# Attention scores of one block as two products of 64 rows and 256 columns, in halves of two PSUM banks

## What is computed

```
D      = exp(log_D - max_log_D)          # log_D from cumulated gates, lower triangle only
qk     = einsum('bhsd,bhtd->bhst', q, k / sqrt(32))
C      = qk * D
h      = (C / (max(|sum C|, exp(-max_log_D)) + 1e-6)) @ v
x      = x + head_layernorm(h) * weight
```

## Time and profile before

| | |
|---|---|
| median of 3 runs | 730.92 us |
| profiled execution | 726.55 us, span 724.8 us |
| TensorE matmul busy | 624.0 us, 86% |
| VectorE busy | 475.6 us, 66% |
| ScalarE busy | 316.1 us, 44% |
| GpSimd busy | 328.0 us, 45% |
| first and last score product (L1180) start | 79.8 us, 289.6 us |

### The profile page before, as it was taken

One profiled execution on the slowest core, in us unless ns is written; L12 is line 12 of the kernel. 1 busy time (PEld: TensorE's weight loads), 2 busy tenths in 40 slices (PEclk: granted clock), 3 DMA queues, 4 the chain that ended last, 5 costly groups with the idle time before them and its releaser, 6 DMA issues.

```text
span 724.8 us, 14827 instructions
## 1 busy us (share of the span) xinstructions
PE 624.0 (86%) x3464; PEld 484.7 (67%) x3481; DVE 475.6 (66%) x943; ACT 316.1 (44%) x704; POOL 328.0 (45%) x328
## 2 busy tenths in 40 slices
PE   3873699999999999613299999999999999999993
PEld 1331366677677666511178888888888888888883
DVE  3664367677656636889657676776777676676673
ACT  3453445355344324300045555545555555555551
POOL 2223534536336433217535555555555455455542
PEclk9997699799689658655599999999999999999998
DMA  9995554555645632260113333333333333333332
GB/s 272 294 297 173 158 159 152 177 158 164 183 124 160 182 99 87 79 259 0 30 32 60 59 47 57 59 47 56 59 50 53 59 51 52 59 51 52 59 45 23
DMA packets 71530, 76.70 MB, mean 106 GB/s; under 512 B 12686, under 2 KB 63636, under 8 KB 71508
## 3 DMA queue, kind: packets, MB, share of 16 engines
q1 hardware_dynamic: 55508, 50.20, 22.3%
q0 software_dynamic: 15712, 25.73, 19.6%
q10 hardware_dynamic: 288, 0.52, 0.2%
HBM read 53.21 MB, written 23.21 MB: 105 GB/s over the span
## 4 chain that ended last, share of the span: by engine, by line
PE 76%; DVE 8%; issue 5%; DMA 5%; POOL 2%; ACT 2%; SPq 1%; DVEq 0%; ACTq 0%; POOLq 0%
PE bank L1282 10%; PE bank L1284 9%; PE bank L1283 9%; PE bank L1180 9%; PE bank L1194 7%; PE bank L1314 5%; PE bank L1310 5%; PE bank L1311 5%; PE bank L1297 4%; PE bank L1175 3%; DMA qT_scratch<-qt 3%; PE bank L1177 2%; PE bank L1269 2%; PE bank L1243 2%; PE bank L1211 1%
## 5 line engine op out<-in xcount | busy, mean ns | idle before, releaser
L1102 POOL DMA_INDIRECT out_rows<-ys,index x71 | 112.9, 1590 | 155.7 <-DVE ys L987 151.9
L1282 PE MATMUL bank<-w12l,xh 128*128 x284 | 120.8, 425 | 2.2 <-DVE xl L959 2.2
L1284 PE MATMUL bank<-w12h,xh 128*128 x284 | 112.5, 396 | 0.0
L1283 PE MATMUL bank<-w12h,xl 128*128 x284 | 112.5, 396 | 0.0
L993 DVE TENSOR_TENSOR w3l<-w,w3h 128x1024 fp32r<-128x1024 f32 x71 | 87.2, 1228 | 30.8 <-issue 29.9
L1194 PEld LDWEIGHTS bank<-aug,c 128*128 128x128 f32 x512 | 77.1, 216 | 36.5 <-issue 31.4
L788 DVE SCALAR_TENSOR_TENSOR c<-bank,d 128x512 f32<-128x512 f32 x64 | 44.2, 690 | 75.1 <-PE bank L1194 66.8
L662 ACT CAST w3h<-w 128x1024 fp32r x71 | 74.4, 1048 | 20.0 <-issue 20.0
L1093 POOL DMA_INDIRECT xg<-token_table,index x71 | 70.4, 991 | 23.8 <-issue 21.0
L1180 PE MATMUL bank<-qbd,kt 128*128 128x512 f32 x128 | 78.2, 697 | 3.4 <-issue 3.4
L1310 PE MATMUL bank<-w3l,hth 128*128 128x256 f32 x284 | 76.4, 302 | 1.8 <-DVE w3l L993 1.8
(11 more groups left out here) (165 smaller groups left out, 1128.2 us busy)
## 6 DMA issues: line engine op xcount, KB each, us to landing
x<-in_x SPq DMA_DIRECT2D x32, 256.0 KB, 3.0
wst<-in_w12T POOLq DMA_DIRECT2D x26, 256.0 KB, 3.5
aug<-in_ctxv SPq DMA_DIRECT2D x16, 264.0 KB, 3.0
ct<-in_ctxT SPq DMA_DIRECT2D x16, 256.0 KB, 4.6
qT_scratch<-qt SPq DMA_DIRECT2D x16, 256.0 KB, 3.7
kt<-in_ctxT SPq DMA_DIRECT2D x16, 256.0 KB
qbd<-qT_scratch SPq DMA_DIRECT2D x64, 64.0 KB
out_rows<-x SPq DMA_DIRECT2D x16, 256.0 KB, 2.2
```

Of the source, the lines that this page charges most:

```text
L1102: q.indirect_dma_start(out=out, out_offset=bass.IndirectOffsetOnAxis(ap=index[:, j:j + 1], axis=0), in_=YS[o][:], in_offset=None, compute_ ...
L1282: mm(acc, XH[i][:, k, :], wl, start=(k == 0), stop=False)
L1283: mm(acc, XL[i][:, k, :], wh, start=False, stop=False)
L1284: ins = mm(acc, XH[i][:, k, :], wh, start=False, stop=(k == NK - 1))
```

## The change

Banks 2 and 3 become one tensor `bank23` of two banks. The scores of a block are two fp32 products: rows 0 to 63 (heads 0 and 1 of the group) with the 256 columns of these heads, into the first half of bank 2, and rows 64 to 127 with the other 256 columns into the first half of bank 3. What is left out of the old product was zero by the block diagonal. Every block uses the same two halves, so the scores of block k now wait for the combine of block k-1. The combine reads both halves in one instruction.

```diff
-        bank = [stack.enter_context(nc.psum_tensor(f"bank{i}", [P, 512], F32)) for i in range(8)]
+        bank = [stack.enter_context(nc.psum_tensor(f"bank{i}", [P, 512], F32)) for i in range(2)]
+        bank23 = stack.enter_context(nc.psum_tensor("bank23", [P, 2, 512], F32))
+        bank += [bank23[:, 0, :], bank23[:, 1, :]]
+        bank += [stack.enter_context(nc.psum_tensor(f"bank{i}", [P, 512], F32)) for i in range(4, 8)]
...
-                        v.scalar_tensor_tensor(C[n % 2][:], bank[2 + n % 2][:], KS, D[n % 2][:],
+                        v.scalar_tensor_tensor(C[n % 2][:].rearrange("p (r q) -> p r q", r=2), bank23[:, :, 0:2 * P],
+                                               KS, D[n % 2][:].rearrange("p (r q) -> p r q", r=2),
                                                ALU.mult, ALU.mult).then_inc(c_ready, 1)
...
-                    wait(pe, c_ready, k - 1)
-                    mm(bank[2 + n % 2][:], KT[i][:, hg, c * P:(c + 1) * P],
-                       QBD[i][:, hg, :, c * P:(c + 1) * P], start=True, stop=True).then_inc(s_ready, 1)
+                    wait(pe, c_ready, k)
+                    for r_ in range(2):
+                        rows_ = slice(r_ * 2 * DH, (r_ + 1) * 2 * DH)
+                        ins = mm(bank23[:, r_, 0:2 * P], KT[i][rows_, hg, c * P:(c + 1) * P],
+                                 QBD[i][rows_, hg, r_ * 2:(r_ + 1) * 2, c * P:(c + 1) * P], start=True, stop=True)
+                    ins.then_inc(s_ready, 1)
```

## The result

| | before | after |
|---|---|---|
| median | 730.73 us | 836.38 us (836.15 to 837.18) |
| profiled execution's span | 724.8 us | 834.2 us |
| first to last score product | 79.8 to 289.6 us | 81.1 to 396.0 us |

The ratio is 1.1455, 95% interval 1.1373 to 1.1537: far slower, and above the range. Executions of one kernel differ by how long TensorE's clock is low; a ratio here compares the faster executions of each kernel, a median takes all of them.

What follows compares the result with a forecast made beforehand. The prediction took TensorE's stream and its clock to bound the attention stage. From 726.55 us, 8.4 for full-clock batches gave 735.0, and 14 for more low-clock stretches gave 749 us; the 8-in-10 range was 710 to 795.

Steps and rivals of the forecast that it cites:

- The clock's term: TensorE in the attention stage: new holes bring one to two more low-clock stretches, costing 14 us.
- I take one to two more of them: 14: Extra low-clock stretches of mean length 20.5 us in the attention stage, 9.6 us each; 14 us taken.
- the holes of 0.29 and 0.41 us: TensorE idle before scores 1 and scores 3 of every full-clock batch, waiting for VectorE's combine.
- the sum: Per full-clock batch, borders, overlap gain and waits over four score blocks: 0.64 us more; at low clock nothing.
- low clock for most of the stage: Rival, chance 0.13: attention stage at the low clock for two thirds of its time, 797 us.
- The 8.4 us for batches at full clock: Attention stage: 13.2 full-clock batches, each 0.64 us longer, add 8.4 us, giving 735.0 before any clock change.
- I take a quarter saved: Score products: only one pass of each overlaps, so 0.86 becomes 0.64 us, gaining 0.22, or 0.43 at low clock.
- The bound of 0.43: Score products of a block: 0.43 us at full clock if the two row halves work side by side in full.
- Borders: Row-group changes entering and leaving the scores: 0.10 to 0.19 us each, 0.30 a block, 0.40 at low clock.
- The wait: Scores wait for the previous combine: 0.29 us at scores 1, 0.41 at scores 3, none at low clock.
- The x2t waits as the start of low stretches: TensorE's waits for x2t, 0.31 to 0.55 us, preceded all three low stretches; a fourth wait had none behind it.
- The rule of the Trainium skill on idling between groups of matmuls: Brief TensorE idling between matmul groups over cycled banks makes the clock oscillate; it favoured 749 us and above.

Runs made afterwards that it cites:

- 767.66: Changed kernel, first exponent product zero-padded from 27 to 64 rows, half-row pair right behind it, mask product last, so no added borders: 767.66 us, ratio 1.0601.
- 732.56: Changed kernel without added borders (exponent product padded to 64 rows, pair behind it, mask last), its half-row pair widened to 512 columns per half: 732.56 us.
- the kernel padded to 128 rows: Kernel before, its first exponent product padded with zero rows from 27 to 128, leaving no row-group border in the attention: 709.75 us, ratio 0.9646.

## Why the prediction was wrong

- **The clock's term** failed. "I take one to two more of them: 14" held the right direction and a tenth of the 135 us that the low clock cost. The reason given for it was wrong too: the holes of 0.29 and 0.41 us don't bring the clock down (727.91 us with them alone). The added borders do most of it, which stood in the sum only at their own 0.10 to 0.20 us each (69 of the 106 us came back without them), and the scores' shorter columns do the rest (35 us between 767.66 and 732.56). The prediction asked what would make the clock fall; in the changed kernel it was low from the start and never rose. The rival "low clock for most of the stage" had the outcome at two thirds and 797 us; it was all of it, 836.
- **Sixteen batches at the low clock** account for the time. By the prediction's own rows, 13.2 x (21.80 - 11.56) = 135 us more, less 16 x 1.02 = 16 for the batch that got shorter: 119 against 110 measured between the profiled executions (836.15 and 726.55). Part of the rest is that the first batches hold less work (18.21 us from 102.90 to 121.11 in the changed kernel, where a full one takes 20.78). The 8.4 us for batches at full clock never came up, since none ran there.
- **Overlap:** "I take a quarter saved" was wrong; a half was. The prediction let only one pass of each product run beside one of the other; the traces have both passes in pairs. The bound of 0.43 was the right end.
- **Borders:** 0.10 at the values' side and with bf16 loads was read rightly (a block of the kernel without them is 0.20 shorter). At the low clock I took 0.40 a block; 0.6 was measured.
- **The wait:** its place and size were right: 0.31 at scores 1, a second one at scores 3, none at the low clock. It made a full-clock batch 0.9 longer rather than 0.70, as the waiting product's first load isn't in advance either.
- **The x2t waits as the start of low stretches:** they aren't needed for one. Without any, a stretch of 34 us remained. But they did stand before three of the stretches of the kernel before and all four of the kernel padded to 128 rows, and the kernel with the 8-column product of 128 rows, which has none, has no low stretch at all. No run took the waits away and left all else, so their share is not settled.

The Trainium skill, "TensorE: Matmul & The Clock Gate", Part 3, has matmuls of different row groups start 4 ns apart; the paired starts here, within 0.01 us of each other, agree, for fp32 too. The Trainium skill, "TensorEngine Tiling (Array Packing)", Key Properties, says that a change of tiling mode drains TensorE; the 0.28 us for two borders agree, and the trace adds what it does to the clock. The rule of the Trainium skill on idling between groups of matmuls, from the section on psum-queue depth-cycling that the prediction weighed, did not decide: here a clock fell with TensorE busy 100% of the windows.

What stays open is why a border weighs more on the clock than a hole of twice its length. The runs show that it does, not how: with borders (12.27 us in an early batch) the clock fell after 44 us and stayed low for the rest of the stage; with holes (12.06 us) it held for 104 us and came back from its one fall.

## What to carry to other kernels

Where TensorE bounds a stage, first ask which clock its stream will be granted: a change that takes array time out can lose far more by it than it saves (135 us against 16 here), and adding full-row products (706 and 711 us against about 730), or padding a short contraction to 128 rows (710), can win. Look also at the clock with which a stage begins: here it was low at the start, and what decided was whether it rose. Count the changes of row group in the stream, and keep products of one row group together. Split a contraction by rows only where it adds no such change, and measure it even then: without added changes the split was still 6% slower than the kernel before (767.66 us).

## What the runs showed of the hardware

- Two fp32 products on the two row halves run fully side by side: 0.43 us a pass pair at 1.2 GHz, starts within 0.01 us.
- A change of row group costs 0.10 us with bf16 loads and 0.14 with fp32 ones at 2.4 GHz, up to 0.30 at 1.2 GHz.
- A product of 8 columns on 64 rows, 64 times in the kernel, took the time from about 730 to 869 us (822 to 905); the same on 128 rows gave 711.
- Half of the score columns, at full rows, made the kernel 2.9% slower, with more waits for x2t; half of them in the half-row pairs, 35 us.
- The clock can stay at 1.2 GHz with TensorE busy throughout: 296 us of 296 in the kernel with the 64-row, 8-column product.
